# Time mixing with group norm and gate projection inside the scan, mixing products packed on 96 rows, value halves in other buffers

## The reference, cut to what matters

```
xn = layernorm(x);  sx = shift(xn) - xn
xxx = tanh((xn + sx*maa_x) @ maa_w1)            # 5 x 32 columns
x5  = xn + sx*(maa_stack + xxx @ maa_w2)        # five mixed inputs
w = exp(-exp(time_decay + tanh(x5[1] @ decay_w1) @ decay_w2))
r, k, v = x5[3] @ Wr.T, x5[0] @ Wk.T, x5[2] @ Wv.T
g = silu(x5[4] @ Wg.T)
scan over tokens, 32 heads of 16x16 state s:
    out = r . (u*k*v + s);   s = k*v + w*s
att = groupnorm per head of out, * gn_w + gn_b
x = x + (att*g) @ Wo.T
```

## Time and profile before

| | us |
|---|---|
| runs (3): median, lowest, highest | 3397.3, 3393.78, 3401.28 |
| the profiled execution, its own time | 3398.43 |
| its span, first to last instruction | 3396.3 |
| busy PE, DVE, ACT, POOL | 3121.7 (92%), 1942.4 (57%), 1169.6 (34%), 396.5 (12%) |
| mean granted TensorE clock | 0.961 of full |
| time mixing, from start to the last store's issue | 1063.2 |

### The profile page before, as it was taken

The page is one execution under the profiler, slowest core; times in us unless marked ns, Lnnn a source line. Parts: engine busy times, 40 slices in busy tenths (PEclk is TensorE's granted clock), DMA queues, the critical chain, the costliest instruction groups (busy, mean ns, idle before and its releaser), DMA issues.

```text
span 3396.3 us, 42256 instructions
## 1 busy us (share of the span) xinstructions
PE 3121.7 (92%) x15120; PEld 2408.3 (71%) x15120; DVE 1942.4 (57%) x2861; ACT 1169.6 (34%) x2544; POOL 396.5 (12%) x220
## 2 busy tenths in 40 slices
PE   6878878887885979999999999999999999999899
PEld 3534533533533758888888888787888888888787
DVE  5796696596597754444454444646444464444544
ACT  4203202202202534343444434434444344434332
POOL 0260260160160000000010000101000010000100
PEclk8897997997997989999999999999999999999999
DMA  2001001001002241111111111112111111111011
GB/s 94 25 0 39 0 1 39 0 0 39 0 0 101 74 148 60 50 34 50 52 39 50 34 49 34 56 49 72 50 45 45 50 35 50 34 49 46 19 45 61
DMA packets 52142, 145.75 MB, mean 43 GB/s; under 512 B 4992, under 2 KB 6528, under 8 KB 50912
## 3 DMA queue, kind: packets, MB, share of 16 engines
q1 hardware_dynamic: 52064, 144.77, 12.7%
HBM read 132.17 MB, written 12.58 MB: 43 GB/s over the span
## 4 chain that ended last, share of the span: by engine, by line
PE 60%; DVE 2%; ACT 1%; issue 0%; DMA 0%; ACTq 0%; DVEq 0%
PE ca_ps L59 17%; PE ca_ps L61 17%; PE ca_ps L60 17%; PE ca_ps L1593 3%; PE ca_ps L1577 3%; PE ca_ps L1585 2%; PE ca_ps L1619 1%; DVE ca_stats L67 0%; DVE ca_xres L1354 0%; DVE ca_ctx_lo L1385 0%; DMA ca_xres<-in_ctxT 0%; ACT ca_q L1129 0%; DVE ca_wq_lo L1312 0%; ACT ca_sk L1270 0%; DVE ca_h_lo L1379 0%
## 5 line engine op out<-in xcount | busy, mean ns | idle before, releaser
L1354 DVE TENSOR_TENSOR ca_xres<-ca_xres,ca_ps 128x512 f32<-128x512 f32 x384 | 263.8, 687 | 244.0 <-PE ca_ps L61 239.1
L1141 ACT ACTIVATE ca_pr<-ca_ps,ca_nb 128x129 f32<-128x129 f32 x512 | 181.8, 368 | 510.4 <-DVE ca_nb L1337 510.3
L59 PE MATMUL ca_ps<-ca_h_hi,ca_wq_hi 128*128 128x512 f32 x768 | 313.4, 408 | 11.6 <-ACT ca_q L1129 6.9
L443 DVE TENSOR_TENSOR_SCAN tm_xn<-tm_wd,tm_vb 128x512 f32<-128x512 f32 x256 | 298.4, 1207 | 13.0 <-DVE tm_vb L438 0.5
L61 PE MATMUL ca_ps<-ca_h_hi,ca_wq_lo 128*128 128x512 f32 x768 | 302.5, 394 | 0.0
L60 PE MATMUL ca_ps<-ca_h_lo,ca_wq_hi 128*128 128x512 f32 x768 | 300.4, 391 | 0.0
L59 PE MATMUL ca_ps<-ca_wv_hi,ca_ctx_hi 128*128 128x256 f32 x1024 | 297.7, 291 | 0.0
L61 PE MATMUL ca_ps<-ca_wv_hi,ca_ctx_lo 128*128 128x256 f32 x1024 | 287.3, 281 | 0.0
L60 PE MATMUL ca_ps<-ca_wv_lo,ca_ctx_hi 128*128 128x256 f32 x1024 | 287.1, 280 | 0.0
L59 PE MATMUL ca_ps<-ca_wo_hi,ca_ct_hi 128*128 128x512 f32 x640 | 253.5, 396 | 0.2 <-DVE ca_xres L1354 0.2
L60 PE MATMUL ca_ps<-ca_wo_lo,ca_ct_hi 128*128 128x512 f32 x640 | 252.7, 395 | 0.0
(11 more groups left out here) (237 smaller groups left out, 6615.2 us busy)
## 6 DMA issues: line engine op xcount, KB each, us to landing
ca_sq<-in_wq SPq DMA_DIRECT2D x49, 512.0 KB, 5.4
ca_so<-in_wo SPq DMA_DIRECT2D x48, 512.0 KB, 3.6
ca_sk<-in_wk SPq DMA_DIRECT2D x33, 512.0 KB, 6.4
ca_sv<-in_wv SPq DMA_DIRECT2D x32, 512.0 KB, 3.7
ca_bvr<-in_bvb SPq DMA_DIRECT2D x32, 256.0 KB, 3.9
tm_xq<-in_x SPq DMA_DIRECT2D x5, 1024.0 KB, 7.6
tm_gg<-in_l0w SPq DMA_DIRECT2D x4, 1024.0 KB, 4.9
tm_rr<-in_x SPq DMA_DIRECT2D x4, 1024.0 KB, 5.1
```

Of the source, the lines that this page charges most:

```text
L59: pe.matmul(out, lhs[0], rhs[0], start=first, stop=False)
L443: v.tensor_tensor_scan(state[t % 2][:, d, :], wd[:, g].rearrange("p b t -> p (b t)"), pair[:, d, :], 0.0, ALU.mult, ALU.add).then_inc(scan ...
L1141: ins = act.activation(pr[hd][:, b, :], ps[:, BANK_SC + b // 2, o:o + KW], ACT.Exp, bias=nbs[hd][:, b:b + 1], scale=SCALE, accum_out=sms[h ...
L1354: v.tensor_tensor(xres[U.h][:, U.quad * 4 + b, :], xres[U.h][:, U.quad * 4 + b, :], ps[:, BANK_O + b % 2, :], ALU.add).then_inc(o_out, 1)
```

## The change

Inside `time_mix`:

1. **Gate projection and group norm go into the scan.** Stage 5 is gone; `gate(f, half)` multiplies the same 48 matmuls chunk by chunk into `pj[1]`, in steps 8f+8 and 8f+9 for f = 0, 1, 2 and after step 31 for f = 3, with Silu per chunk on ACT (step 8f+11). The group norm is done per chunk: `centred(f)` (one fp32 matmul by I − mean) in step 8f+10, Square and scaling by `gn_w` on ACT (8f+12), `variance(f)` (8f+12), Sqrt (8f+14), a 128x128 reciprocal on DVE (8f+14), `unpacks(f)` (8f+14), `gated(f)` on DVE (8f+15: multiply, then one instruction for + gn_b, · g), `hi` and `lo` (8f+17). Chunk 3 follows the scan, between the four parts of the output projection, which accumulates into `vb`.
2. **The value halves** are `v_hi` (in `xq`'s memory) and `v_lo` (in `gg`'s), so `x_hi`/`x_lo` keep the gate's input. Only chunk 0's halves and the r·u·k products stand ahead of the scan; the halves of chunks 1 to 3 and the four bonus multiplications of DVE go into steps 0 to 5.
3. **Mixing products of j = 2 to 5 are packed.** `h5` and `h4` are split into hi and lo, and POOL issues 12 DMAs a quad (32x512 each) that lay hi, hi, lo of each block on 96 rows of `packed`; one fp32r matmul against `lora2p` (hi, lo, hi of the weights) replaces the fp32 matmul. j = 1 stays as it was.
4. **The rest.** `xT` is transposed into `pj`/`mx`; the next x is loaded in four DMAs as the scan frees `v_hi`; the next quad's statistics come after the scan, its normalisation after the last `lo`. Quad 3 is written out too, so the loop is quads 1 and 2; POOL's loop is written out. In quad 0 `lora2p` is made by one more ACT and one more DVE instruction.
5. In `cross_attend`, `query` into the key bank no longer waits for ACT's evacuation of the query before it.

```diff
-                    if m < 4:
-                        lhs, rhs = lora2[32 * m:32 * m + 32, c * P:(c + 1) * P], h5[32 * m:32 * m + 32, :]
-                    else:
-                        lhs, rhs = lora2e[:, c * P:(c + 1) * P], h5e[:]
+                    if j == 1:
+                        lhs, rhs = lora2[32:64, c * P:(c + 1) * P], h5[32:64, :]
+                    else:
+                        if c == 0 and j == 2:
+                            pe.wait_ge(pack_in[0], q * 48 + 48)
+                        elif c == 0:
+                            pe.wait_ge(pack_in[1], q * 144 + 144)
+                        lhs, rhs = lora2p[:, j - 2, c * P:(c + 1) * P], packed[:, j - 2, :]
...
+            def pack(s, m):
+                hi, lo = (h5_split[32 * m:32 * m + 32, 0, :], h5_split[32 * m:32 * m + 32, 1, :]) if m < 4 else (
+                    h5_split[0:LORA, 2, :], h5_split[0:LORA, 3, :])
+                for k, part in enumerate((hi, hi, lo)):
+                    gp.dma_start(packed[32 * k:32 * k + 32, s, :], part).then_inc(pack_in[min(s, 1)], 16)
...
+                def gated(f):
+                    v.wait_ge(unpacked, q * 4 + (f + 1))
+                    v.wait_ge(cent_out, q * 8 + (2 * f + 2))
+                    v.tensor_tensor(vv[:, f, :, 1:L + 1], vv[:, f, :, 1:L + 1], quad3(pj[0][:]), ALU.mult).then_inc(y_ready, 1)
+                    b_ = VEC["gn_b"] + f
+                    v.wait_ge(g_ready, q * 4 + (f + 1))
+                    v.wait_ge(y_ready, q * 8 + (2 * f + 1))
+                    v.scalar_tensor_tensor(out=vv[:, f, :, 1:L + 1], in0=vv[:, f, :, 1:L + 1], scalar=vec[:, b_:b_ + 1],
+                                           in1=quad3(gg[:, f, :]), op0=ALU.add, op1=ALU.mult).then_inc(y_ready, 1)
...
                 for t in range(STEPS):
                     spread(t + 2)
                     if t >= 1:
                         accumulate(t - 1)
+                    if t == 2:
+                        bonus(3)
+                    for f in range(3):
+                        if t in (8 * f + 8, 8 * f + 9):
+                            gate(f, t - (8 * f + 8))
+                        if t == 8 * f + 10:
+                            centred(f)
+                        if t == 8 * f + 12:
+                            variance(f)
+                        if t == 8 * f + 14:
+                            unpacks(f)
+                gate(3, 0)
+                gate(3, 1)
+                accumulate(STEPS - 1)
...
+                output(0)
+                centred(3)
+                output(1)
+                variance(3)
+                output(2)
+                unpacks(3)
+                output(3)
...
-                pe.wait_ge(q_out, C.n * 2 + hd)
+                pe.wait_ge(q_out, C.n * 2 + (hd if bank == BANK_Q else 0))
```

More of the change, by code:

```diff
@@ L257, in roots, with quad @@
                 act.activation(std[:, :], mv[:, :, 1], ACT.Sqrt, bias=eps[:]).then_inc(std_ready, 1)
-            def quad(q, first):
+            def quad(q, first, last):
                 def hi(j, c):
@@ L355, in _ @@
             roots(0)
             split_w(0)
[L357 to L360 removed]
+            act.wait_ge(first_in, 16 * (len(FIRST) + 2))
+            quads(act, quad)
         @block.vector
@@ new lines, in decay, with bonus, spread @@
+                    pe.matmul(pj[(1 + f) % 2][:], dec2[:, f * P:(f + 1) * P], dh, start=True, stop=True).then_inc(decay_full, 1)
+                def bonus(c):
+                    pe.wait_ge(ruk_ready, q * 4 + (c + 1))
+                    if c == 3:
+                        pe.wait_ge(bonus_used, q * 4 + 1)
+                    pe.matmul((pj[0], pj[1], mx[1], pj[0])[c][:], head_sum[:], sx[:, c, :], start=True, stop=True).then_inc(bonus_full, 1)
+                def spread(t):
+                    if t >= STEPS:
+                        return
+                    g = t // 8
+                    if t % 8 == 0:
+                        pe.wait_ge(v_split_ready, q * 4 + (g + 1))
+                    if t < 2:
+                        pe.wait_ge(f_free, q * 12 + (8 + 2 * t + 2))
+                    else:
+                        pe.wait_ge(scanned, q * (3 * STEPS) + 3 * (t - 1))
+                    for e in range(2):
+                        d = 2 * (t % 8) + e
+                        pe.matmul(vb[:, 2 * (t % 2) + e, :], spread_v[:, d, :], v_hi[:, g, :], start=True, stop=False)
+                        ins = pe.matmul(vb[:, 2 * (t % 2) + e, :], spread_v[:, d, :], v_lo[:, g, :], start=False, stop=True)
+                    ins.then_inc(vb_full, 1)
@@ new lines, in gate @@
+                def gate(f, half):
+                    if half == 0:
+                        if f == 0:
+                            pe.wait_ge(bonus_used, q * 4 + 2)
+                            pe.wait_ge(split_ready, q * (4 * J) + 4 * J)
+                        else:
+                            pe.wait_ge(g_ready, q * 4 + f)
+                        if first and f == 0:
+                            pe.wait_ge(w_ready, 7)
+                    for c in (2 * half, 2 * half + 1):
+                        ins = mm3(pe, pj[1][:], [t[:, 3, c, f * P:(f + 1) * P] for t in (w_hi, w_lo)], (x_hi[:, c, :], x_lo[:, c, :]),
+                                  c == 0, c == EC - 1)
+                    if half == 1:
+                        ins.then_inc(g_full, 1)
@@ new lines, in unpacks, with output @@
+                def unpacks(f):
+                    pe.wait_ge(grstd_ready, q * 4 + (f + 1))
+                    for b in range(4):
+                        ins = pe.matmul(pj[0][:, b * L:(b + 1) * L], unpack[:, b, :], grs[:], start=True, stop=True)
+                    ins.then_inc(unpacked, 1)
+                def output(c):
+                    pe.wait_ge(y_split_ready, q * 4 + (c + 1))
+                    for b in range(4):
+                        ins = mm3(pe, vb[:, b, :], (y_hi[:, c, b, :], y_lo[:, c, b, :]),
+                                  (w_hi[:, 4, c, :], w_lo[:, 4, c, :]), c == 0, c == EC - 1)
+                        if c == EC - 1:
+                            ins.then_inc(wo_full, 1)
```

649 lines of the change are left out of this document (370 added, 279 removed).

## The result

The changed kernel takes **3282.4 us**, the median of four runs (3279.23 to 3285.89), beside 3395.5 us for the kernel before on the same chip: a ratio of 0.9668, with a 95% interval of 0.9646 to 0.9689. The forecast was 3286, in a range of 3250 to 3335.

What follows compares the result with a forecast made beforehand. DVE was taken to bound the scan, PE stages 2 to 5. Gains of 80.1 (three cycles), 12.7 (quad 0), 12.5 (last tail) and 6.9 (query) make 112.2 off 3398.4: 3286 us, range 3250 to 3335.

Steps and rivals of the forecast that it cites:

- The cycle before, 258.8: Old kernel, one quad's last scan to the next quad's: parts read from the trace sum to 258.8 us, 259.4 measured.
- The scan, 130.6: A quad's 32 scan steps: from 116.0 to about 130.6 us, 10.9 of inserted DVE work and 3.7 of lock waits.
- The collision: In the scan, second instruction of `gated` waits 1.85 us for POOL's product, both reading SBUF; twice a quad, 3.7 us.
- PE at nothing in the scan: In the scan, PE's added work costs nothing: eight steps need 27.4 us of PE against DVE's 28.8 and more.
- The fourth rival, one copy after another: POOL's packed copies each start only when the one before has landed, 4.7 us each: 3455 us in all; chance 3%.
- Stage 2 to scan, 44.8: PE's stage 2 to scan: 73.0 us less 11.1 for stage 5, 8.6 for packed products, 8.5 for scan entry.
- The tail, 24.8: A quad's last scan to the next quad's first `sx`: from 35.4 to about 24.8 us, by PE's alternating order.
- The loop's return, 2.5: Where the quad loop returns, DVE waits 2.5 us for instructions, in one place instead of two.
- Quad 0, 12.7: Quad 0 gains 31.9 us ahead of its scan, loses 14.6 in it, 1 in copies, about 3.6 for `lora2p`: 12.7.
- The query's wait, 6.9: Cross attention: PE's wait for the query's evacuation, 6.9 us, counted as gained in full because PE is bound there.
- the rivals with 3350 and 3526 us: Group-norm hand-offs in the scan become visible, +48, copies +16: 3350, 20%. PE's scan clock halves, 240 in all: 3526, 1%.
- The one with 3259: No DVE-POOL lock in the scan, 4 x 3.7 us, and up to 12 us fewer stage-end hand-offs: 3259; 15%.

Runs made afterwards that it cites:

- the short reciprocal: Changed kernel with the in-scan reciprocal of group-norm statistics for chunks 0 to 2 done on one of 128 columns: 3274.6 us, ratio 0.964.
- the later gating: Changed kernel with the second instruction of `gated` for chunks 0 and 1 moved one scan step later: 3264.1 us, ratio 0.9616.
- The doubled gate: Changed kernel with the gate matmuls of chunks 0 to 2 inside the scan issued twice, 36 more a quad: 3304.2 us, ratio 0.9734.

## Why the prediction was right, point by point

The likeliest case came about, its mechanisms in the scan with it; the total is closer than the parts, which miss in both directions. By spans, with 119.0 us gained where 112.2 were forecast:

| us gained | predicted | measured |
|---|---|---|
| quad 0, to its last scan | 12.7 | 6.9 |
| three cycles | 80.1 | 87.8 (778.3 to 690.5) |
| last tail | 12.5 | 11.7 (store issued 23.7 after the last scan, before 35.4) |
| behind time mixing | 6.9 | 12.7 |

- **The cycle before, 258.8.** I put it together from parts of different cycles, and it came near the mean of 259.4 by luck. On the mean of the three cycles, stage 2 to scan gained 25.4 us and not 28.2 (28.5 in quad 2, from which I read it, 25.1 and 22.7 in the others). `sx` to tanh, which I called unchanged, gained 2.0.
- **The scan, 130.6.** Measured 127.7 to 131.0, mean 129.5. That an insertion on DVE costs its length was shown by the short reciprocal.
- **The collision.** Shown by moving the instruction. I had 1.85 us a case and it is about 1.65 (2.39 less 0.74). The slip: I wrote that the instruction ends one undisturbed length after POOL. By the earlier trace rows it is 1264.13 less 1263.58, 0.55 us; here it is 406.34 less 405.80, 0.54. In exchange I missed its second price, PE's clock behind the longer wait. I also left chunk 2 out: it collides behind the last scan, and what that costs was not tried.
- **PE at nothing in the scan.** True, but with little to spare. Four waits of about 0.4 us inside the scans are all that shows, and all four are gone with the later gating. The doubled gate hid 2.6 us a quad of what it added; how much would fit elsewhere in the scan stays open.
- **Packing.** I had 0.72 us a product. 16 products made 11.2 us by the medians, where I expected 11.5, and 16.6 by the profile, so 0.72 is the lower end.
- **The copies.** I took 1 us a quad and there is none. No row waits for them. The fourth rival, one copy after another, is out.
- **Tanh to stage 2, 19.9.** 18.3 to 18.8. DVE starts 3.0 us after tanh in quad 1 (281.08), not 3.4, and gets through to the end of its multiplication for j = 2, chunk 3, in 15.3 us, not 16.1.
- **Stage 2 to scan, 44.8.** 45.0, 44.5 and 45.3; that it fits this well is in part the luck of the first point. "The first spread within 3 us of stage 4's end" holds with 2.66 us of waiting.
- **The tail, 24.8.** 25.2 and 25.3. Two errors cancelled: the chain to the last halves ends at 18.3 us (260.86 less 242.61), before the 19.5 that I had, and then most of the last product goes at half the clock.
- **The loop's return, 2.5.** Failed: 5.2 us (30.5 less 25.3). The wait itself is 6.5 us (the earlier trace rows had 2.46).
- **Quad 0, 12.7.** Failed by 5.8. I carried the gain of the later quads ahead of the scan, 31.9, over to quad 0. There DVE also makes the low halves of the weights between the stages. PE waits 2.32, 2.84 and 2.78 us for DVE's mixing, where before it waited 1.38 and 1.13: 5.4 us of PE's saving is spent so. The miss is even larger than the table says, for the first `sx` came 1.9 us earlier than before (16.91 against 18.82), and in the edits of the changed kernel it lies anywhere from 15.3 to 19.3. From `sx` to the last scan quad 0 gained 5.0 us. That the weights are the cause is argued from the order of the work, not tried.
- **The query's wait, 6.9.** The mechanism was right and the size too small: 9.4 to 10.0 us, shown by putting it back. I summed PE's waits only and left out the 11.0 us of its weight loads; that these are the difference is argued. Some 3 us of the gain behind time mixing stay unexplained.

Nothing spoke for the rivals with 3350 and 3526 us. The one with 3259 was wrong on the collision. For its other half, fewer hand-offs, there is some support. The cycles gained 7.7 us more than forecast: 3.0 from the copies, 4.0 from tanh to stage 2 and 4.7 in the scan, 0.4 from `sx` to tanh, less 4.0 in the tails with the loop's return and 0.4 from stage 2 to the scan.

## What to carry to other kernels

When one engine bounds a loop, work moved into the loop costs its own length; where in the step it stands decides the rest. Where two SBUF tiles are read by DVE and two by POOL, put DVE's instruction first behind the event that also starts POOL's product: here 2.45 us became 0.73. And look behind each longer wait of PE for its clock: in the tail it cost 1.5 us more for twelve matmuls. A wait's price is to be read from PE and from its weight loads together, and a new helper instruction on ACT is to be looked at for what is queued behind it.

Still open for a further step: the last output product and the residual stand ahead of the next quad's transposes, although only the store needs them. Moving them behind was not tried.
